# A selective scan on one core: float32 inputs to the state, exponents written to PSUM with a stride, and a rebuilt preparation

## The reference

```
xn   = rmsnorm(layernorm(x)) * norm_w              # 2048 x 128
lo, Bs, Cs = split(xn @ x_proj_w.T, [8, 72])       # 8, 64 and 64 columns
dt   = softplus(lo @ dt_proj_w.T + dt_proj_b);  A = -exp(A_log)      # A: 128 x 64
# the rows are cut into 32 chunks of 64 steps, all chunks in parallel, h = 0 at first
h    = exp(dt[..., None] * A) * h + dt[..., None] * bt[:, None, :] * xt[..., None]
y    = sum over the 64 states of h * ct
out  = (y + layernorm(x) * D) @ out_proj_w.T
```

## Time and profile before

| | us |
|---|---|
| median of 3 runs | 1644.42 (1643.6 to 1648.71) |
| the profiled execution | 1653.65 |
| its span | 1651.6 |
| TensorE busy | 1370.3 (83%) |
| VectorE busy | 1037.8 (63%) |
| ScalarE busy | 958.5 (58%) |
| GpSimd busy | 649.1 (39%) |

### The profile page before, as it was taken

How to read it: one execution, slowest core, us unless ns; L and a number is a source line. 1 busy time by engine, 2 the same in 40 slices (tenths; PEclk the granted TensorE clock), 3 DMA queues, 4 the chain that set the end, 5 groups by cost and what they waited for, 6 DMA issues and landing times.

```text
span 1651.6 us, 30294 instructions
## 1 busy us (share of the span) xinstructions
PE 1370.3 (83%) x11160; PEld 917.5 (56%) x11160; DVE 1037.8 (63%) x2050; ACT 958.5 (58%) x1507; POOL 649.1 (39%) x520
## 2 busy tenths in 40 slices
PE   4889996699999987889999996714888888877998
PEld 2667774344444434657666774413666666655676
DVE  5887766877777755786675445513666666665533
ACT  4667773166666676767675442534677677653433
POOL 2756656711222003756553002503566666661000
PEclk9999998699999997999999998755555555557999
DMA  4100000000000000010000000134111101110000
GB/s 139 53 25 1 0 1 1 1 1 2 2 0 1 1 1 26 26 53 1 0 1 1 1 0 0 21 69 73 46 26 25 25 22 25 31 53 1 1 0 25
DMA packets 34316, 32.20 MB, mean 19 GB/s; under 512 B 24200, under 2 KB 27672, under 8 KB 32536
## 3 DMA queue, kind: packets, MB, share of 16 engines
q1 hardware_dynamic: 34200, 30.64, 7.5%
HBM read 24.81 MB, written 5.82 MB: 19 GB/s over the span
## 4 chain that ended last, share of the span: by engine, by line
PE 56%; DVE 14%; ACT 13%; issue 8%; SPq 5%; POOL 2%; DMA 1%; DVEq 0%; POOLq 0%; ACTq 0%
PE ps L595 12%; PE ps L672 7%; PE ps L895 7%; PE ps L682 7%; ACT arena L1149 6%; PE ps L787 4%; PE ps L750 4%; PE ps L868 3%; PE ps L770 3%; DVE maxima L1667 3%; ACT hr L1038 2%; DVE xn L1468 2%; SPq L505 2%; PE ps L881 1%; SPq L499 1%
## 5 line engine op out<-in xcount | busy, mean ns | idle before, releaser
L1149 ACT ACTIVATE arena<-ps 128x512 f32<-128x512 f32 x256 | 244.5, 1080 | 116.4 <-PE ps L868 116.1
L1387 POOL TENSOR_TENSOR arena<-arena 128x512 f32<-128x512 f32 x126 | 223.4, 1793 | 194.9 <-PE ps L895 83.8
L1667 DVE TENSOR_REDUCE maxima<-ps 128x1 f32<-128x512 f32 (+3 forms) x320 | 190.3, 633 | 59.4 <-PE ps L753 39.9
L868 PE MATMUL ps<-arena 12*128 12x64 bf16 x2048 | 136.5, 236 | 101.0 <-DMA arena<-dt_parts 52.8
L595 PE MATMUL ps<-xp,wup 128*128 128x512 f32 (+1 forms) x768 | 207.8, 418 | 13.9 <-ACT hr L1038 10.0
L1411 POOL TENSOR_TENSOR hr<-arena,hr 128x512 fp32r<-128x512 f32 x128 | 173.7, 1363 | 93.8 <-ACT hr L1038 93.6
L595 PE MATMUL ps<-hr,wdn 128*128 128x512 f32 x768 | 201.3, 412 | 8.8 <-DVE hr L1570 7.3
L1104 ACT ACTIVATE arena<-ps 128x1024 f32<-128x1024 f32 (+1 forms) x192 | 150.5, 812 | 73.2 <-PE ps L770 37.0
L1038 ACT ACTIVATE arena<-ps 128x512 f32<-128x512 f32 x256 | 162.5, 635 | 51.0 <-PE ps L595 50.6
L868 PEld LDWEIGHTS ps<-arena 12*128 12x128 bf16 x2048 | 103.7, 121 | 157.1 <-ACT arena L1149 77.1
L595 PEld LDWEIGHTS ps<-xp,wup 128*128 128x128 f32 x768 | 148.3, 200 | 64.3 <-POOL wup L1398 16.4
(11 more groups left out here) (206 smaller groups left out, 2162.6 us busy)
## 6 DMA issues: line engine op xcount, KB each, us to landing
arena<-up_dram SPq DMA_DIRECT2D x16, 256.0 KB, 2.9
arena<-dn_dram SPq DMA_DIRECT2D x16, 256.0 KB, 3.2
arena<-up_dram SPq DMA_DIRECT2D x2, 1024.0 KB, 4.9
arena<-dn_dram SPq DMA_DIRECT2D x2, 1024.0 KB, 7.8
b_parts<-arena SPq DMA_DIRECT2D x16, 96.0 KB
dt_parts<-arena SPq DMA_DIRECT2D x8, 192.0 KB
u_parts<-arena SPq DMA_DIRECT2D x16, 96.0 KB
arena<-dt_parts SPq DMA_DIRECT2D x32, 48.0 KB
```

What stands on the lines that cost most here:

```text
L868: mm = e.matmul(ps[:, 4 + n % 2, j * 64:(j + 1) * 64], aw[32 * r:32 * r + KR, g0 + j, :], dts[k % 2][32 * r:32 * r + KR, g0 + j, :, th * T ...
L1149: e.activation(to.rearrange("p t m d -> p d m t"), ps[:, 4 + n % 2, :].rearrange("p (d m t) -> p d m t", d=DBK, t=TU), ACT.Exp, scale=-1.0 ...
L1387: e.tensor_tensor(hs[:, t % 2, cols], decay[:, u % 2, t4 * W + cols.start:t4 * W + cols.stop], hs[:, 1 - t % 2, cols], ALU.mult).then_inc( ...
L1667: e.tensor_reduce(maxf[:, at_max[0]:at_max[-1] + 1:max(1, at_max[-1] - at_max[0])], ps[:, n % 2, 0:ng * w].rearrange("p (g k) -> p g k", g ...
```

## The change

The text of the scan is rebuilt; the other stages stay, but for a piece of GpSimd work in stage d.

- `spread_bank` writes feature j of a bank to the columns j, j + 8, j + 16, ... and `decay_bank` reads the bank from its first to its last column; its output runs over 8 neighbouring features.
- `inputs` uses float32 operands with 2 rows (the two batches) in place of 12 rows of bf16 parts. u and b are no longer split; chunks of u and b are 4 steps long (TI), those of dt stay 8.
- Three state buffers; a multiply of step t waits for the read-out of step t - 3 and not of t - 2.
- B is projected with 128 columns per 128 rows, from a zero-padded weight `xpb` (one load more at the start); the projections, transposes and ScalarE's copies are interleaved by block of 512 rows; dt's subtractions go to VectorE; ScalarE's dt splits and u copies alternate; the skip term is made last.
- `aw` and `czf` are cleared by GpSimd at the start of the ReLU stage before the scan; `bparts` is gone.
- SyncE stores b in 4 transfers, u in 8, dt in one for chunk 0 and one for the other seven; a chunk of u and b is fetched in 8 transfers, one of dt in 12.

```
-                mm = e.matmul(ps[:, 4 + n % 2, j * 64:(j + 1) * 64], aw[32 * r:32 * r + KR, g0 + j, :],
+                mm = e.matmul(ps[:, 4 + n % 2, j:512:DBK], aw[32 * r:32 * r + KR, g0 + j, :],
                               dts[k % 2][32 * r:32 * r + KR, g0 + j, :, th * TU:(th + 1) * TU], start=True, stop=True)
...
-                    rows = slice(32 * r, 32 * r + KR)
-                    mm = e.matmul(ps[:, r, mm_ * D:(mm_ + 1) * D], bs[k % 2][rows, mm_, t % TC, :],
-                                  us[k % 2][rows, mm_, t % TC, :], start=True, stop=True)
+                    rows = slice(32 * r, 32 * r + B)
+                    mm = e.matmul(ps[:, r, mm_ * D:(mm_ + 1) * D], bs[k % 2][rows, t % TI, mm_, :],
+                                  us[k % 2][rows, t % TI, mm_, :], start=True, stop=True)
...
-            to = decay[:, u % 2, :].rearrange("p (t m d) -> p t m d", t=TU, d=D)[:, :, :, d0:d0 + DBK]
-            e.activation(to.rearrange("p t m d -> p d m t"),
-                         ps[:, 4 + n % 2, :].rearrange("p (d m t) -> p d m t", d=DBK, t=TU), ACT.Exp,
+            to = decayf[u % 2].rearrange("p (t m d) -> p m t d", t=TU, d=D)[:, :, :, d0:d0 + DBK]
+            e.activation(to, ps[:, 4 + n % 2, :].rearrange("p (m t d) -> p m t d", d=DBK, t=TU), ACT.Exp,
                          scale=-1.0).then_inc(SC["decay_ready"], 1)
...
-                        if t >= 2 and n == 0:
-                            e.wait_ge(SC["y_done"], t - 1)
+                        if t >= 3 and n == 0:
+                            e.wait_ge(SC["y_done"], t - 2)
...
+                for b in range(B):
+                    sp.wait_ge(SC["bf_ready"], 2 * b + 2)
+                    store_b(b)
+                for g in range(NTB):
+                    sp.wait_ge(SC["uT_ready"], g + 1)
+                    store_u(g)
+                sp.wait_ge(SC["dt_split"], NTB)
+                store_dt(0, 1)
+                sp.wait_ge(b_out, 16 * 2 * B)
+                sp.wait_ge(u_out, 16 * 2 * NTB)
+                fetch_inputs(0)
+                sp.wait_ge(dt_out, 16)
+                fetch_dt(0)
+                store_dt(1, NC)
+                sp.wait_ge(dt_out, 32)
+                fetch_inputs(1)
...
+            def relu_mixture_pool(e, st, nxt):
+                if nxt and nxt["kind"] == "scan":
+                    e.wait_ge(MX["y_read"], len(gelus) * NTB * E)
+                    e.memset(czf, 0.0).then_inc(SC["zeroed"], 1)
+                    e.memset(aw, 0.0).then_inc(SC["zeroed"], 1)
...
-    scratch = {k: nc.dram_tensor(f"{k}_parts", v, BF16, kind="Internal").ap() for k, v in shapes.items()}
+    scratch = {k: nc.dram_tensor(f"{k}_parts", v, F32 if k in ("u", "b") else BF16, kind="Internal").ap() for k, v in shapes.items()}
```

More of the change, by code:

```diff
@@ L118, in build @@
         xpw = sb("xpw", [P, RANK + 2 * STATE])
+        xpb = sb("xpb", [P, 3 * STATE])
         dtw = sb("dtw", [RANK, D])
@@ L200, in build @@
         aw = carve(GD * P // 2).bitcast(BF16).rearrange("p (g n) -> p g n", n=P)
+        dts0 = carve(GD * NM * TC // 2)
+        decayf = [carve(TU * W) for _ in range(2)]
+        hsf = [carve(W) for _ in range(3)]
+        us1 = carve(TI * 4 * D)
+        bs1 = carve(TI * 4 * P)
         assert top[0] <= kept
@@ L526, in _ @@
[L526 to L538, removed]
@@ new lines, in _ @@
+                sp.wait_ge(SC["dt_split"], NTB)
[8 more added lines that the diff above has]
+                fetch_inputs(1)
+                sp.wait_ge(SC["xn_turned"], NTB)
+                fetch_dt(1)
+                for k in range(2, NI):
+                    sp.wait_ge(SC["in_done"], 3 * TI * (k - 1))
+                    fetch_inputs(k)
+                    if k % 2 == 0 and k // 2 + 1 < NC:
+                        sp.wait_ge(SC["spread_done"], 2 * BKU * (k // 2))
+                        fetch_dt(k // 2 + 1)
@@ L927, in scan_tensor, with rows_b @@
[L927 to L932, removed]
-            e.wait_ge(SC["z_ready"], 4)
+            def rows_b(g):
+                for i in range(TPB * g, TPB * (g + 1)):
+                    half = STATE * (1 - i // 8)
+                    mm = e.matmul(ps[:, 4 + g, i % TPB * P:(i % TPB + 1) * P], ut[:, i * P:(i + 1) * P],
+                                  xpb[:, half:half + P], start=True, stop=True)
+                mm.then_inc(SC["bc_done"], 1)
@@ new lines, in scan_tensor @@
+            turn_rows(0)
+            turn_rows(1)
+            low_rank(0)
+            turn_rows(2)
+            low_rank(1)
+            steps_of(0)
+            turn_rows(3)
+            low_rank(2)
+            steps_of(1)
+            low_rank(3)
+            steps_of(2)
+            rows_b(0)
+            rows_b(1)
+            steps_of(3)
+            rows_b(2)
+            rows_b(3)
+            for h in range(2):
+                e.wait_ge(SC["bf_ready"], h + 1)
+                for b in range(B):
+                    mm = e.matmul(ps[64 * b:64 * b + 64, 4 + h, :], xpw[:, RANK + STATE:RANK + 2 * STATE],
+                                  ut[:, b * S + h * 512:b * S + (h + 1) * 512], start=True, stop=True)
+                mm.then_inc(SC["bc_done"], 1)
@@ L1772, in scan_vector @@
[L1772 to L1780 removed]
+                parts = [slice(g * TB, (g + 1) * TB) for g in range(NTB)]
@@ new lines, in dt_rest @@
+                def dt_rest(n, g, after, done):
+                    e.wait_ge(SC[after], g + 1)
+                    e.tensor_tensor(dt_piece(g), dt_piece(g), dt_part(n, g), ALU.subtract).then_inc(SC[done], 1)
+                z_add(0)
+                for g in range(1, NTB):
+                    z_add(g)
+                    z_size(g - 1)
+                z_size(NTB - 1)
+                for g in range(NTB):
+                    e.wait_ge(SC["ln_ready"], g + 1)
+                    e.scalar_tensor_tensor(out=zt[:, parts[g]], in0=zt[:, parts[g]], scalar=0.0, in1=soft[:, parts[g]],
+                                           op0=ALU.max, op1=ALU.add).then_inc(SC["dt_ready"], 1)
```

298 lines of the change are left out of this document (139 added, 159 removed).

## The result

| | before | after |
|---|---|---|
| median, us | 1645.39 (1643.6 to 1648.71, 4 runs) | 1845.01 (1841.59 to 1847.51, 4 runs) |
| profiled execution, us (its span) | 1653.65 (1651.6) | 1843.85 (1841.8) |
| first to last read-out, us | 373.3 | 585.7 |
| one step, read-outs 3 to 58, us | 5.71 | 9.64 |

The changed kernel takes 1.1209 times as long [1.1182 to 1.1236]: +200 us on the medians and +190.2 between the two profiled executions. The forecast was 1803 with a range of 1695 to 1910. The sign and the main terms came as forecast, but +159 was some 40 us short, because one term of the sum, the strided write, was put at nothing. Between the two profiled executions it was 31 us short, and the loop accounts for that (+212 instead of +178).

The account below looks back on a forecast made before the run. TensorE at 1.2 GHz was taken to bound the scan. Loop +178, preparation through read-out 0 -22 and the memsets' new stage +3 made +159 us on the median of 1644: 1803 us, range 1695 to 1910.

Parts of the forecast that it names:

- the strided write: Exponent matmuls writing PSUM with a stride of 8 floats: taken as nothing; upper bound a doubled pitch, +1.7 us a step.
- Float32 inputs: Scan's input matmuls: two instructions a call, each of twice the columns, 5.12 instead of 1.28, +3.84 us a step.
- Rival D: Scan inputs: more overlap among row groups, group 2 beside 0 and 1, 7.1 us a step, 1696 us; chance 11%.
- Rival C: Scan inputs: float32 weight loads of two row groups queue, +1.7 us a step, 1908 us; chance 8%.
- rival B: Scan exponents: strided PSUM writes slow the matmuls, +1.7 us a step, +101 us, 1904 us; chance 15%.
- half of B: Scan exponents: strided PSUM writes cost half of rival B's price, 1854 us.
- The end of the loop: Scan loop of 551 us: 59 steps of 8.8 us, then four without exponents at 7.9 us each.
- The exponential: ScalarE's 512-column exponential: 0.6 us a bank in a stream instead of 0.86; worth nothing in the loop, first 17 -4 us.
- Preparation: Stretch before the scan loop: first exponents at 1076 instead of 1102 us, -26, bounds -12 and -35; read-out 0 at 1098.
- Memsets: GpSimd's memsets: two moved to the start of the stage two before, -8 us in preparation, about +3 there.
- The stall in step 2: Scan step 2: the stall of 20 us for transfers goes, the second chunk's fetch waiting for 2 stores, not 24 more.
- Rival A: Scan: TensorE's clock rises to 2.4 GHz, 4.7 to 5.3 us a step, 1563 us; chance 10%.

Follow-up runs that it names:

- experiment 4: The changed kernel with input matmuls reading only the upper bf16 half of each float of u and b: 1614.33 us, 5.84 us a step.
- experiment 10: The changed kernel with end-to-end exponent writes and all sixteen input calls issued together after the third bank, row groups in turn: 1671.27 us.
- experiment 1: The changed kernel with exponents written end to end again, ScalarE reading with a step of 64 columns and still writing runs of eight: 1794.64 us.
- experiment 3: The kernel before with only ScalarE's loop order changed, so that it writes runs of eight: 1613.19 us, 0.9783 of before.
- experiment 6: The changed kernel with bf16 inputs and end-to-end exponent writes, multiplies waiting for the read-out of step t - 2: 1570.08 us; 1568.52 with t - 3.
- experiment 7: The changed kernel with four unused 128x128 bf16 matmuls of 256 columns added before each read-out: 1879.32 us, 10.2 us a step.
- experiment 12: The kernel of experiment 10 with two banks of exponents before the inputs and two behind the read-out: 1656.53 us, 6.41 us a step.
- experiments 2 and 4: The first: the kernel before with strided exponent writes and ScalarE's runs of eight, 1656.39 us. The second: see experiment 4.

## Why the prediction was right, and where it was short

**The bound.** TensorE at 1.2 GHz was taken for the bound and is: busy in 529.70 of 530.02 us, against 4.90 of 5.71 per step before. The waits for ScalarE, 35.8 us, went to 0.3, as forecast.

**Float32 inputs, +3.84 us a step.** 3.80 by experiment 4. So close a match is in part luck: in experiment 4 TensorE waits 7.0 us for ScalarE in 55 steps (0.13 a step), so that its own work for the float32 inputs is nearer 3.9. The pace, 0.213 an instruction, and the assumption that row groups 2 and 3 stay one behind the other were right. Rival D's mechanism exists, but the order of issue forbids it: where the calls of all groups are issued in turn (experiment 10) they overlap fully. Rival C (two groups' weight loads queue) is refuted by the same trace, and by the changed kernel's: its sign was more than 1.8 us for groups 0 and 1, and they fill 1.86, but so does group 2 alone, and C would have had 3.4.

**The strided write, taken as free.** This is the step of the prediction that failed. The reason given, that 1.2 GHz leaves twice the time per column, was worth nothing; the pitch doubled, as the upper bound had it. Its price was half of rival B's, 0.82 instead of 1.7 us a step and 50 us instead of 101 by experiment 1, for the reason shown there. The prediction had the case "half of B" at 1854; it came to 1845.

**The end of the loop.** The forecast was 551 us and it took 585.7. Up to read-out 58 it took 1658.55 - 1100.17 = 558.4 instead of 58 x 8.8 = 510 (+48, the stride's 0.8 a step). From there it took 27.3 instead of 8.8 + 31.6 = 40.4 (-13), so that 13 of the 48 us were hidden by luck. The last step holds no inputs and takes 1.7 us instead of 7.9. The steps without exponents were priced too high, since 4 x 0.21 taken off 8.8 leaves more than inputs (5.12) and a read-out (1.87) need. And without exponents between, the inputs of groups 2 and 3 partly overlap, 32 instructions in 4.05 us, which the chain of waits shows:

```profile
1678.29 1.86 PE ps L901 x32
1680.16 4.05 PE ps L887 x32
1684.20 3.26 PE ps L901 x64
```

**The exponential**, 1080 to an estimated 600 ns: 596. Worth nothing on this path, as forecast, but 35 us in the kernel before (experiment 3: 1647.72, the kernel before in the same series, to 1613.19), where TensorE's waits for ScalarE fell from 35.8 us to 10.1.

**Preparation.** First exponents forecast for 1076, seen at 1075.77; dt split about 1061, its store issued at 1062.18; read-out 0 forecast for 1098 (1101 with the +3 of stage d), seen at 1100.17. From the first exponents to read-out 0 it took 24.4 us against 18.3, where 22 was forecast. The first sixteen exponentials hardly got shorter:

```profile
1078.15 1.08 ACT L1179 ACTIVATE arena<-ps 128x512 f32<-128x512 f32 x2
1079.87 1.09 ACT L1179 ACTIVATE arena<-ps 128x512 f32<-128x512 f32 x2 [0.63 <-PE ps L874]
```

A pair starts every 1.72 us, where two took 2 x 0.86 before (14.94 us for 17), because ScalarE waits 0.63 us for TensorE's next two banks. In experiment 1 a pair starts every 1.29 us, so that the strided writes cost 8 x 0.43 = 3.4 of the 4 us that were forecast as gained.

**Memsets.** The cost in stage d was put at +3 and came to 2.9: there VectorE's L1548 is held for 4.68 us, until GpSimd's memsets end (898.04 and 898.01), and the kernel that ran 1.2 us ahead of the one before at the last GpSimd add (889.85 against 891.02) is 1.8 us behind it at the scan's start (L1796's predecessors at 1022.55 against 1020.78). The gain, -8, is the instruction at 1024.37: 0.17 us instead of 8.25.

**The stall in step 2** is gone; steps 0 to 3 took 9.95, 8.75, 9.62 and 10.71 us. **Three state buffers**: nothing, by experiment 6.

**Rival A** (clock rises) did not happen in the changed kernel. The Trainium skill (TensorE: Matmul & The Clock Gate, The HAM clock gate) says that sustained activity releases the throttle; 530 us of TensorE without a gap, with matmuls of 2 and 12 rows and read-outs with 32-column weights, did not raise it. Why experiment 7 got short stretches at a higher clock, and why they ended, is open.

## What to carry to other kernels

When a change moves work onto the engine that is the bound, price it in that engine's instruction starts: float32 doubled the starts and their length here, and no gain on ScalarE could pay for it. If one engine's access pattern must be scattered, find out which of the two sides is cheap: reading PSUM 64 columns apart cost ScalarE nothing, writing it in lone floats doubled TensorE's pitch. And when matmuls use only some rows of the array, issue the row groups in turn, all of them, before making any of them cheaper: experiment 12 is 138 us below experiment 1 by order alone.

## What the runs showed of the hardware

- A matmul that writes lone floats to PSUM takes twice as long per column (0.107 against 0.053 us for 64 columns at 1.2 GHz), at a step of 2 as of 8; pairs that start at an even column cost nothing. Two row groups writing lone floats to different banks still go side by side.
- Four row groups of float32 matmuls run side by side, each at 0.213 us an instruction of 128 columns, two of them per call, at 1.2 GHz.
- ScalarE: 512 columns from PSUM took 1080 ns with lone floats written and 596 with runs of eight, whether PSUM was read end to end or 64 columns apart.
- GpSimd memsets held a small VectorE instruction for 4.68 us in one place and 8.25 us in another, each time until a memset ended; without a memset beside it the second took 0.17 us.
- bf16 inputs with 2 rows instead of 12 left the step as it was (5.84 us in experiments 2 and 4).
- TensorE without a gap for 530 us kept its clock at 0.50; with matmuls on 128x128 weights added it rose for some 10 us at a time, with a mean of 0.78 and 0.90 over the stretches shown, and fell again without a gap.
